# Second cross attention in groups of four tiles on row and column groups of TensorE, in whole fp32

## What is computed

```python
q = (queries @ Wq).reshape(b, s, KV_HEADS, GROUP, HEAD_DIM)   # 8, 4, 16
k = (keys @ Wk).reshape(b, s, KV_HEADS, HEAD_DIM)
v = (values @ Wv).reshape(b, s, KV_HEADS, HEAD_DIM)
scores = jnp.einsum('bqhgd,bkhd->bhgqk', q, k) * scale
attn = jax.nn.softmax(scores, axis=-1)
out = jnp.einsum('bhgqk,bkhd->bqhgd', attn, v)
return out.reshape(b, s, EMBED) @ Wo
```

## Time and profile before

| | before |
|---|---|
| median of 3 runs | 2521.13 us (2520.95 to 2522.86) |
| profiled execution, its own time | 2521.75 us |
| its span in the trace | 2520.0 us |
| TensorE busy | 2432.5 us, 97% of the span |
| VectorE, ScalarE, GpSimd busy | 1293.5, 934.5, 731.2 us |
| mean granted clock of TensorE | 0.99 |

### The profile page before, as it was taken

How to read it: one execution, slowest core, us unless ns; L and a number is a source line. 1 busy time by engine, 2 the same in 40 slices (tenths; PEclk the granted TensorE clock), 3 DMA queues, 4 the chain that set the end, 5 groups by cost and what they waited for, 6 DMA issues and landing times.

```text
span 2520.0 us, 39518 instructions
## 1 busy us (share of the span) xinstructions
PE 2432.5 (97%) x13371; PEld 2072.9 (82%) x13371; DVE 1293.5 (51%) x3008; ACT 934.5 (37%) x2499; POOL 731.2 (29%) x433
## 2 busy tenths in 40 slices
PE   5999899999999999999999999999999999998997
PEld 3788788888888988887888888888888888876665
DVE  6444644444444544456644444444444444567675
ACT  2111344444444444442233333333333333336772
POOL 4434423222232222222211111111111111126770
PEclk9999999999999999999999999999999999998998
DMA  3110211111121111211111111111111111100000
GB/s 114 67 47 28 92 70 64 50 67 50 50 83 50 51 66 50 73 44 36 34 44 44 44 44 44 44 44 44 44 44 44 44 44 44 54 7 1 1 1 34
DMA packets 36976, 119.49 MB, mean 47 GB/s; under 512 B 4920, under 2 KB 7352, under 8 KB 36928
## 3 DMA queue, kind: packets, MB, share of 16 engines
q1 hardware_dynamic: 36928, 118.88, 13.8%
HBM read 116.76 MB, written 2.10 MB: 47 GB/s over the span
## 4 chain that ended last, share of the span: by engine, by line
PE 89%; DVE 4%; issue 3%; POOL 2%; ACT 1%; SPq 0%; DMA 0%; POOLq 0%; DVEq 0%; ACTq 0%
PE pj L553 19%; PE pj L554 18%; PE pj L555 18%; PE ou L553 6%; PE ou L555 6%; PE ou L554 6%; PE pv L731 2%; PE sc L868 2%; PE pv L877 2%; PE sc L715 2%; PE tp L983 1%; PE tp L722 1%; PE sc L553 1%; POOL w_lo L417 1%; POOL w_hi L415 1%
## 5 line engine op out<-in xcount | busy, mean ns | idle before, releaser
L409 POOL TENSOR_TENSOR w_lo<-raw,w_hi 128x1024 fp32r<-128x1024 f32 x145 | 347.1, 2394 | 1436.6 <-ACT w_hi L1090 1396.1
L553 PE MATMUL pj<-xt_hi,w_hi 128*128 128x512 f32 (+2 forms) x1296 | 516.9, 399 | 8.8 <-POOL w_lo L417 2.5
L554 PE MATMUL pj<-xt_lo,w_hi 128*128 128x512 f32 (+2 forms) x1296 | 500.1, 386 | 0.0
L555 PE MATMUL pj<-xt_hi,w_lo 128*128 128x512 f32 (+2 forms) x1296 | 499.1, 385 | 0.0
L553 PEld LDWEIGHTS pj<-xt_hi,w_hi 128*128 128x128 f32 x1296 | 244.7, 189 | 54.0 <-issue 3.8
L555 PEld LDWEIGHTS pj<-xt_hi,w_lo 128*128 128x128 f32 x1296 | 244.1, 188 | 49.4
L554 PEld LDWEIGHTS pj<-xt_lo,w_hi 128*128 128x128 f32 x1296 | 245.1, 189 | 41.2
L553 PE MATMUL ou<-w_hi,act_hi 128*128 128x512 f32 x684 | 273.8, 400 | 4.2 <-DVE act_lo L1820 2.1
L555 PE MATMUL ou<-w_hi,act_lo 128*128 128x512 f32 x684 | 267.5, 391 | 0.0
L554 PE MATMUL ou<-w_lo,act_hi 128*128 128x512 f32 x684 | 266.7, 390 | 0.0
L1363 DVE TENSOR_TENSOR x<-x,ou 128x512 f32<-128x512 f32 (+1 forms) x192 | 130.9, 685 | 255.0 <-PE ou L555 254.7
(11 more groups left out here) (256 smaller groups left out, 4836.9 us busy)
## 6 DMA issues: line engine op xcount, KB each, us to landing
raw<-in_l1a_w SPq DMA_DIRECT2D x80, 512.0 KB, 4.2
raw<-in_l0x_w SPq DMA_DIRECT2D x64, 512.0 KB, 4.1
side<-in_side SPq DMA_DIRECT2D x32, 512.0 KB, 4.1
raw<-in_ffn_w SPq DMA_DIRECT2D x15, 512.0 KB, 3.3
raw<-in_l1x_w SPq DMA_DIRECT2D x7, 512.0 KB, 3.4
raw<-in_l0f_w SPq DMA_DIRECT2D x6, 512.0 KB, 3.8
raw<-in_taylor_w SPq DMA_DIRECT2D x5, 512.0 KB, 7.1
x<-in_x SPq DMA_DIRECT2D x2, 1024.0 KB, 6.7
```

What stands on the lines that cost most here:

```text
L409: pool.tensor_tensor(WL[:, s, :], RAW[:, s, :], f32(WH[:, s, :]), ALU.subtract).then_inc(w_ready[s], 1)
L553: pe.matmul(out, wh, xh, start=first, stop=False)
L554: pe.matmul(out, wh, xl, start=False, stop=False)
L555: return pe.matmul(out, wl, xh, start=False, stop=last)
```

## The change

The 64 tiles become 16 groups of 4 (`NG`, `KG`). A group is one batch and one half of the key/value heads; its four tiles lie on partitions 0-31, 32-63, 64-95 and 96-127.

- Scores: eight whole fp32 matmuls of 256 columns with 32 contraction rows each, two for each of four row groups, into four banks (`sc0`, `sc1`, `pj0`, `pj1`). Keys are no longer split and are repeated twice in place of four times, so `keys` has 2 blocks for each half of the batches in place of 4. The scale 1/4 moves into the copy of the queries, the negation into the row maximum (`negate=True`).
- Transposes: as before, but into two banks by turns (`tp`, `ou1`). ScalarE copies each to a whole fp32 tile `turned_whole`; VectorE's low parts of the turned probabilities go.
- Values: four whole fp32 matmuls of 512 columns per group, each with 32 output rows on one column group of `pv`, in place of an `mm3` for each tile.
- Queries: 8 blocks of 512 columns (two halves of the batches) in place of 16 of 256. `queries(1, c)`, for the second half, stands after group 5, group 6 and (two of them) group 7.
- VectorE's low parts of keys, values and queries go. Two of four pieces of the 3-bit weights are dequantised between layer norm 4 and the first row maximum. Two of the four weight transposes of the last layer stand ahead of the last `output`.
- The output and the head split before it stay as they were.

```diff
-            for s in WK_SLOTS:
-                ready(s, SLOT["l1x"][s])
+            ready(3, SLOT["l1x"][3])
...
-            pe.wait_ge(x_done, OU["l1x"])
-            keys(0, 2)
-            keys(0, 3)
...
-            turn(4, range(0, 2))
-            for m in range(2, KC):
-                pe.wait_ge(kr_lo, m - 1)
-                keys(1, m)
-            turn(4, range(2, B))
...
+            def scores(n):
+                b, part = n // 2, n % 2
+                pe.wait_ge(kx_ready, n + 1)
+                pe.wait_ge(q_out, b // HB * KC + 2 * part + 2)
+                if n:
+                    pe.wait_ge(lx_exp, n * KG)
+                else:
+                    pe.wait_ge(pj_done, PJ["ln4"] + B)
+                for h in range(2):
+                    for g in range(KG):
+                        r = slice(32 * g, 32 * g + 32)
+                        at = (2 * part + h) * HALF + b % HB * S
+                        last = pe.matmul(score_banks[g][:, h * 256:(h + 1) * 256], AF[r, at:at + S], KX[r, n % 2, :],
+                                         start=True, stop=True)
+                        if h:
+                            last.then_inc(gs_full, 1)
+            def transposes(n, g):
+                t = n * KG + g
+                pe.wait_ge(lx_pn, t + 1)
+                if t >= 2:
+                    pe.wait_ge(tn_out, t - 1)
...
+            def values(n):
+                b, part = n // 2, n % 2
+                pe.wait_ge(tn_out, (n + 1) * KG)
+                pe.wait_ge(pad_ready, n + 1)
+                if part == 0 and b:
+                    pe.wait_ge(on_done, b)
...
+                for g in range(KG):
+                    at = part * P + 32 * g
+                    last = pe.matmul(pv[32 * g:32 * g + 32, :], pads(b)[:, at:at + 32], TW[:, g, :],
+                                     start=part == 0, stop=part == 1)
+                last.then_inc(pg_full, 1)
...
+            for n in range(NG):
+                transposes(n, 0)
+                if n + 1 < NG:
+                    scores(n + 1)
+                for g in range(1, KG):
+                    transposes(n, g)
+                if n % 2 == 0 and n:
+                    output(n // 2 - 1)
+                values(n)
+                for c in {5: (0,), 6: (1,), 7: (2, 3)}.get(n, ()):
+                    queries(1, c)
+            turned_weights(0)
+            turned_weights(1)
+            output(B - 1)
...
+            for n in range(NG - 1):
+                turned_out(n, 0)
+                turned_out(n, 1)
+                if n == 6:
+                    queries(1, 0)
+                exps(n + 1, 0)
+                turned_out(n, 2)
+                exps(n + 1, 1)
+                turned_out(n, 3)
+                exps(n + 1, 2)
+                if n % 2:
+                    heads(n // 2)
+                exps(n + 1, 3)
```

More of the change, by code:

```diff
@@ L73, in halves @@
         half(None, (last, 1))
-def pairs(engine, pair):
-    pair(0, True, False)
-    with engine.Fori(1, B // 2 - 1) as i:
-        pair(i, False, False)
-    pair(B // 2 - 1, False, True)
 def starts(order, per):
@@ L1035, in _, with queries @@
-            pairs(pe, pair)
-            pe.wait_ge(w_deq, 12)
-            for c in range(KC):
+            def queries(hf, c):
+                n = hf * KC + c
+                bank = ou[0] if hf else query_banks[c]
+                if n == 0:
+                    pe.wait_ge(x_done, OU["l1x"])
+                if n == 2:
+                    pe.wait_ge(kr_out, 3)
+                if n == 3:
+                    pe.wait_ge(q_out, 1)
+                if n in (4, 5):
+                    pe.wait_ge(x_done, OU["l1x"] + n - 2)
+                if n in (6, 7):
+                    pe.wait_ge(q_out, n)
+                for k in range(KC):
+                    w = both(W, lambda t: wpair(t, WQ_SLOTS, k, 512)[:, c * P:(c + 1) * P])
+                    last = mm3(bank[:], w, wide(XT, hf)(k), k == 0, k == KC - 1)
+                last.then_inc(q_full, 1)
@@ new lines, in output @@
+            def output(b):
+                pe.wait_ge(on_done, b + 1)
+                pe.wait_ge(x_done, OU["l1x"] + b)
+                pe.wait_ge(q_out, 4 if b < 2 else 5 if b == 2 else 8)
+                if b == 0:
+                    ready(4, SLOT["l1x"][4])
+                    ready(3, SLOT["l1x_o"])
+                for c in range(KC):
+                    last = mm3(ou[0][:], both(A, lambda t: t[:, ON1 + c * P:ON1 + (c + 1) * P]),
+                               wrows(WO_SLOTS)(c), c == 0, c == KC - 1)
+                last.then_inc(ou_full, 1)
@@ L1044, in _ @@
                 last.then_inc(pj_full, 1)
+            turn(4, range(0, 4))
+            pe.wait_ge(pj_done, PJ["ln4"] + HB)
+            for s in WQ_SLOTS:
+                ready(s, SLOT["l1x"][s])
+            queries(0, 0)
+            turn(4, range(4, 6))
+            queries(0, 1)
+            turn(4, range(6, B))
+            queries(0, 2)
+            scores(0)
+            queries(0, 3)
+            for n in range(NG):
[12 more added lines that the diff above has]
+            output(B - 1)
+            turned_weights(2)
+            turned_weights(3)
             layer_norm(5)
@@ new lines, in _ @@
+            queries(0, 0)
+            turned(4, range(6, B))
+            queries(0, 1)
+            queries(0, 2)
+            weight_hi(3, SLOT["l1x_o"])
+            exps(0, 0)
+            queries(0, 3)
+            for g in range(1, KG):
+                exps(0, g)
+            for n in range(NG - 1):
+                turned_out(n, 0)
[10 more added lines that the diff above has]
+                exps(n + 1, 3)
+                if n == 6:
+                    queries(1, 1)
+                if n == 7:
+                    queries(1, 2)
+                    queries(1, 3)
@@ L1952, in _, with row_max, row_recip @@
-            pairs(dve, pair)
-            for c in range(KC):
+            normed(4)
+            def row_max(n, g):
+                dve.wait_ge(gs_full, n * KG + g + 1)
+                dve.tensor_reduce(NM[:, g, :], score_banks[g][:].rearrange("p (h s) -> p h s", h=GQ),
+                                  axis=AX.X, op=ALU.max, negate=True).then_inc(lx_nm, 1)
+            def row_recip(n, g):
+                t = n * KG + g
+                at = slice(g * GQ, (g + 1) * GQ)
+                dve.wait_ge(lx_exp, t + 1)
+                dve.reciprocal(RC[:, at], SUMS[:, at]).then_inc(lx_rc, 1)
```

452 lines of the change are left out of this document (174 added, 278 removed).

## The result

The changed kernel took 2493.07 us (median of 4 runs, 2491.09 to 2495.64) beside 2521.99 us (2520.95 to 2526.05) for the kernel before: a ratio of 0.9883, 95% interval 0.9866 to 0.9900, so 29 us less. A second comparison gave 2493.57 beside 2524.49, 0.9877 (0.9862 to 0.9892). The forecast was 2502 us with a range from 2468 to 2530. The profiled execution took 2491.09 us, the lowest of the four; its span is 2489.3.

A forecast was written before the change was run, and what follows sets the result against it. TensorE was taken to bound the kernel before, ScalarE most of each new group. First group's end 2278, stage 171, end 14 and rest 37.3 sum to a 2500.3 us span, 2502 us with 1.75 around it; range 2468 to 2530.

The forecast's parts named there:

- Row groups side by side, and column groups too: A group's four score products, and its four values products, run at the same time: 0.85 us each, not 3.4.
- columns one after another: Rival, chance 0.13: values products run serially, 3.4 us in place of 0.85; stage 195 us, total 2529, slower by 8.
- The chain of a group: Scores wait for the last exponential, then ScalarE bounds from its second copy: periods 8.7 and 9.2, mean 9.0 us.
- The second half's queries: Four query blocks of 2.7 us behind the values of groups 5, 6 and 7 add 7 us to the stage.
- The clock: Waits bring the clock down about half the time: stage 142 us at full clock, 200 at lower, 171 taken.
- The start: Removed keys give 5.5 us: first scores at 2267.6, first exponentials at 2271, first group's exponentials end at 2278.
- The end and the rest: From last exponentials to the last layer norm's rows 14 us, before 17.2; the following 37.3 us stay.
- full clock throughout: Rival, chance 0.14: the gaps do not bring the clock down in the stage; total 2471 us.
- in order: Rival, chance 0.04: records start in program order, scores take 9 steps and values 5; 28 us more, total 2530.
- lower clock nearly throughout: Rival, chance 0.07: TensorE's work in a period is never dense enough to raise the clock; total 2536 us.

The follow-up runs named there:

- the filler: 12 unread fp32r matmuls of 512 columns added to the changed kernel ahead of the values in groups 1, 3, ..., 13: 2483.54 us, ratio 0.9840.
- the blocks: Changed kernel with the four removed key blocks done again for nothing (48 matmuls), run twice: 2496.01 us, ratio 0.9884, and 2494.76 us, ratio 0.9876.

## Why the prediction was right, and where not

- *Row groups side by side, and column groups too.* Right: 1.07 and 1.00 us, where I took 0.85 for each with 0.2 for a start. Shown by undoing each: +48 us for the rows, +33 for the columns. The Trainium skill ("TensorE: Matmul & The Clock Gate", Part 3, The mechanism) has matmuls on tiles start and end in program order. Here 16 score records need four steps of 0.2 to 0.3 us, so the second record of a product doesn't hold back the next row group's first; with the records in program order it would have been nine, as in the rival. Taken product by product, though, the four started in the order of the queue (7 ns apart), so the case that the sentence doesn't fit is that of the separate matmuls in the earlier trace rows. The rival "columns one after another" was wrong as a case; its price was 195 us of stage and 2529 in all, and built, it measured 190.2 and 2527.17. That is closer than its working: it had every group late, where every second one kept its 9.1 us and the others took 14.8, and its head copy's wait of 2.2 us was 2.4 at the full clock but 4.0 and more in the other cases. (By its own terms its 173 at the full clock is 172.)
- *The chain of a group.* The places were right: scores wait for the last exponential, ScalarE is the bound from its second copy on, and TensorE's wait ahead of the values, 3.1 us in the forecast, was 3.05. Periods were 9.1 and 9.6 where I had 8.7 and 9.2: the read of the last row sum (0.2 us) and 0.2 more until the second copy. Against the mean of 9.0 that went into the sum this is 4.4 us over 15 periods.
- *The second half's queries.* +7 expected; with the filler, at the full clock, their three periods are 8.5 us over the others (10.6, 11.4, 14.2 against 9.1, 9.6, 9.1). So the whole stage at the full clock is 148 us, not 142.
- *The clock.* The step that failed. I took half of the time at the lower clock and 12 us a period there, 20 us for the queries: 58 us for a stage all at the lower clock, 29 for the half. In the trace 45 of 158 us are at the lower clock, 29%, and they cost 10 (158.4 less 148). The share was too high, but the price more so: I had output products at the lower clock (5.2 us) push the values and the next scores late. They never did: the clock was back by the output's first matmuls, and what was left is ScalarE's 1.4 us of longer wait. Of the 12.6 us between 171 and 158.4, the clock makes 19 and the two items above give 6 back, so the stage's total is nearer than its parts by luck. That the wait ahead of the values is what brings the clock down was right, and is shown by the filler: with these waits filled, the low-clock time went from 45 to 11 us.
- *The start.* First scores at 2270.24, predicted 2267.6; first exponentials at 2273.3, predicted 2271; end of the first group's exponentials 2279.5, predicted 2278. Keys priced at 5.5 gave 0.5 at this place: the wait that replaced them brought the clock down, and the queries behind it ran at 1.2 GHz. Filling three waits there brought 3.5 us back: with the clock up both with the blocks (24.0) and without them (20.0), the blocks cost 4.0 at this place. The first row maximum also stood behind VectorE's two dequantised pieces and began 1.2 us after the scores' last record ended (2271.39); no run takes these pieces away, so their part stays open. I had written of the clock in the stage and of "a stretch at the lower clock" for 1 us here; it was 3.5.
- *The end and the rest.* 14 predicted, 14.1 measured; 37.3 and 37.3.
- *Rival "full clock throughout"*, 2471: the fillers come near its condition and give 2483.5; its price had the 142 in it. The rivals "in order" (28 us more) and "lower clock nearly throughout" did not come: the scores take four steps, and the clock was low for 29% of the stage.
- The sum by steps: 2278 + 171 + 14 + 37.3 predicted, 2279.5 + 158.4 + 14.1 + 37.3 measured.

## What to carry to other kernels

A chain that moves from TensorE to another engine leaves waits on TensorE, and a wait has two prices: its length, which may be free, and the lower clock behind it. Price that second part only by the TensorE work that stands on the chain at that moment (here scores and one transpose, 1.4 us a group), not by all of TensorE's work. Work that must be done anyway belongs into such waits: the same four query blocks, moved from the chain into the wait, took 10 us off, by the chain that they left and by the clock; 84 useless matmuls took off the same by the clock alone.

Here, grouping products with a contraction of 32 rows or an output of 32 by four paid only because the four lie on different row or column strips; the same grouping without it lost 41 us.

## What the runs showed of the hardware

- Four whole fp32 products on four row groups took 1.07 us for 2 x 256 columns each, one after another 3.53 (3.3 times); on four column groups 1.00 us for 512 columns each, one after another 3.54 (3.5 times).
- In the run with the 22 matmuls at the start, the clock fell at 2253.5 us, in a wait of 1.32 us that stood behind one of 1.37 and 0.9 us of transposes. With 5 matmuls more behind each of the first two pairs of rows it held until 2275.6.
- The changed kernel has eight waits of 2.9 to 3.05 us ahead of values. The clock fell during one of them or at most 1.3 us behind it in six cases, for 3.4 to 10.2 us, and did not fall behind those that ended at 2336.61 and 2425.54. A query block of 12 matmuls stood right behind the values of 2336.61, but also behind those of 2358.64, where the clock fell, and not behind those of 2425.54. What decides it stays open. The values that ended the waits at 2358.64 and 2425.54, and the clock behind each:

```profile
2358.64 1.76 PE L995 MATMUL pv<-turned_whole,values_padded 128*32 128x512 f32 x8 [3.05 <-ACT turned_whole L1317]
2359.00:2362.00 3.00, 3.00 (x12) 1.39 (x5) 0.87 (x2) 2.54 (x14) 1.47 (x2) 0.50 0.00 0
...
2425.54 1.07 PE L995 MATMUL pv<-turned_whole,values_padded 128*32 128x512 f32 x8 [3.05 <-ACT turned_whole L1317]
2426.00:2438.00 12.00, 8.85 (x68) 5.63 (x60) 5.57 (x13) 10.57 (x52) 5.54 (x6) 1.00 0.01 2
```

- What stands ahead of the changed stage varies from one execution to the next by more than the small edits bring: layer norm 4's aggregation began at 2249.08 us in one profiled execution of the changed kernel and at 2253.18 in the other, while the stage behind it agreed within 0.1 us. Distances inside a trace tell such edits apart where start times don't.
